# Patch embedding in token rows: pixels stationary, weights moving, in a fused embedding, attention and feed-forward kernel

## The reference

```
h = patches(x) @ W_embed + b_embed + pos_embed      # 196 x 256 for each image
h = concatenate([h, txt], axis=1)                   # 228 x 256
h = h + attention(layernorm(h))                     # 16 heads of 16, causal, then @ Wo.T + bo
h = h + ffn(layernorm(h))                           # ternary up 256 -> 1024, gelu, ternary down
```

## Time and profile before

| what | before |
|---|---|
| median of three runs | 2072.05 us |
| the profiled execution | 2070.54 us |
| its span in the profile | 2068.8 us |
| mean granted clock of TensorE | 0.978 |
| TensorE busy | 94% of the span |
| VectorE, ScalarE, GpSimd busy | 73%, 63%, 43% |

### The profile page before, as it was taken

How to read it: one execution, slowest core, us unless ns; L and a number is a source line. 1 busy time by engine, 2 the same in 40 slices (tenths; PEclk the granted TensorE clock), 3 DMA queues, 4 the chain that set the end, 5 groups by cost and what they waited for, 6 DMA issues and landing times.

```text
span 2068.8 us, 61840 instructions
## 1 busy us (share of the span) xinstructions
PE 1939.4 (94%) x25986; PEld 1574.5 (76%) x25986; DVE 1514.4 (73%) x2849; ACT 1296.2 (63%) x2050; POOL 887.8 (43%) x1069
## 2 busy tenths in 40 slices
PE   2889999999999999999999999999999999999875
PEld 2668788778778777777877877887787787777664
DVE  5457778778777777777877777787777777777753
ACT  2346666666666666666666666666666666666652
POOL 1124444444444544443444444444444445444443
PEclk8789999999999999999999999999999999999987
DMA  4111111011111101111111111110111111010000
GB/s 133 26 44 40 50 53 49 29 49 40 53 49 53 48 26 49 44 50 52 49 40 39 44 49 49 54 49 28 50 40 53 49 54 46 28 49 22 29 29 23
DMA packets 62989, 93.85 MB, mean 45 GB/s; under 512 B 9634, under 2 KB 59270, under 8 KB 59768
## 3 DMA queue, kind: packets, MB, share of 16 engines
q1 hardware_dynamic: 62712, 89.90, 15.7%
HBM read 45.03 MB, written 14.94 MB: 29 GB/s over the span
## 4 chain that ended last, share of the span: by engine, by line
PE 71%; DVE 20%; issue 4%; ACT 3%; POOL 1%; DMA 1%; DVEq 0%; SPq 0%; POOLq 0%; ACTq 0%
PE dense L327 41%; PE score L327 17%; PE pvps L327 7%; PE dense L384 2%; DVE st L942 2%; DVE rs L914 2%; DVE mx L954 2%; DVE km L990 2%; PE dense L345 2%; DVE h L938 2%; DVE pT_lo L904 2%; PE dense L373 2%; DVE h L1030 1%; DVE mr L966 1%; DVE aT_lo L908 1%
## 5 line engine op out<-in xcount | busy, mean ns | idle before, releaser
L1161 POOL TENSOR_SCALAR_AFFINE_SELECT pr<-pr 114x456 f32<-114x456 f32 x512 | 311.9, 634 | 899.9 <-ACT pr L668 899.9
L668 ACT ACTIVATE pr<-score 114x1368 f32<-114x1368 f32 x256 | 335.7, 1311 | 302.2 <-PE score L327 301.9
L953 DVE TENSOR_REDUCE mx<-score 114x4 f32<-114x456 f32 x256 | 161.4, 630 | 187.3 <-PE score L327 187.1
L954 DVE TENSOR_REDUCE mx<-score 114x4 f32<-114x912 f32 x256 | 281.1, 1098 | 0.0
L327 PE MATMUL dense<-wdn,g 128*114 128x256 bf16 x1024 | 241.0, 281 | 3.5 <-issue 3.5
L1180 POOL TENSOR_TENSOR acc<-acc,sq 128x456 f32<-128x456 f32 x192 | 229.2, 1194 | 18.9 <-POOL acc L1180 0.4
L327 PE MATMUL dense<-wdn,gl 128*114 128x256 bf16 x1024 | 235.1, 275 | 0.0
L327 PE MATMUL score<-km,qs 32*114 32x114 f32 (+1 forms) x4096 | 221.7, 331 | 7.8 <-ACT pr L668 7.6
L327 PE MATMUL pvps<-pr,vp 114*32 114x228 f32 (+1 forms) x4096 | 204.6, 317 | 0.5 <-ACT raw L740 0.5
L914 DVE RECIPROCAL rs<-rs 128x228 f32<-128x228 f32 x128 | 200.8, 1568 | 0.0
L327 PE MATMUL score<-qs,km 32*114 32x228 f32 (+1 forms) x4096 | 196.4, 308 | 0.0
(11 more groups left out here) (135 smaller groups left out, 4423.4 us busy)
## 6 DMA issues: line engine op xcount, KB each, us to landing
pix<-x SPq DMA_DIRECT2D x32, 1176.0 KB
rs<-raw SPq DMA_DIRECT2D x256, 57.0 KB, 2.0
cx<-raw SPq DMA_DIRECT2D x256, 57.0 KB, 2.0
out<-h SPq DMA_DIRECT2D x64, 228.0 KB
h<-txt SPq DMA_DIRECT2D x32, 64.0 KB, 8.0
km<-wqkvo SPq DMA_DIRECT2D x1, 1024.0 KB, 15.4
h<-w_upT SPq DMA_DIRECT2D x1, 1024.0 KB, 14.5
km<-w_embed SPq DMA_DIRECT2D x1, 768.0 KB, 10.3
```

The lines of the kernel that those rows point to most:

```text
L668: act(pr[q % 2][:], score[0:R, :, 0:SW], ACT.Exp, scale=float(HD) ** -0.5).then_inc(a["exp"], 1)
L953: nc.vector.tensor_reduce(mx[:, b, 0, :, r], score[0:R, :, 0:R], AX.X, ALU.max)
L954: nc.vector.tensor_reduce(mx[:, b, 1, :, r], score[0:R, :, R:SW], AX.X, ALU.max).then_inc(v["max"], 1)
L1161: nc.gpsimd.affine_select(out=blocks, in_=blocks, compare_op=ALU.is_ge, fill=0.0, base=0, pattern=[[0, 4], [1, R]], channel_multiplier=-1) ...
```

## The change

The pixels become the stationary operand and the weights the moving one. `embed(pair, blk, ph)` now works on a block of token rows: for each image `b` and each colour it loads 114 (block 0) or 82 (block 1) patches of `pT` as stationary columns and moves 256 columns of `we`. The result has tokens in the partitions already. `hidden_columns`, the tile `hT`, `hidden_rows` and the semaphores `pe["emb"]` and `a["emb"]` are gone. `("ht", 0)` and `("ht", 1)` take the places of `("emb", 0)` and `("emb", 1)` in `DENSE`; the old places of `ht` and the spare place are gone. `embed(t, 1, 1)` moves from the end of stage 3 to stage 4, where `hidden_rows` stood. `hidden(t, hs, 0)` moves on VectorE from stage 4 to stage 2, behind the two `lo_part`.

```diff
-         ("pix", 5), ("emb", 0), ("x2t", 0), ("x2t", 1), ("up", 0), ("up", 1), ("up", 2), ("up", 3), ("up", 4),
-         ("up", 5), ("up", 6), ("up", 7), ("emb", 1), ("ht", 0), ("ht", 1), ("v", 1), ("mt", 0), ("spare", 0), ("dn", 0),
+         ("pix", 5), ("ht", 0), ("x2t", 0), ("x2t", 1), ("up", 0), ("up", 1), ("up", 2), ("up", 3), ("up", 4),
+         ("up", 5), ("up", 6), ("up", 7), ("ht", 1), ("v", 1), ("mt", 0), ("dn", 0),
...
-            def embed(pair, m, ph):
+            def embed(pair, blk, ph):
...
-                    eng.wait_ge(*emptied(pair, "emb", m))
+                    eng.wait_ge(*emptied(pair, "ht", blk))
                 eng.wait_ge(v["pix"], count(6, pair, 3 * ph + 3))
-                o = bank_of("emb", m)[:, 0:TP].rearrange("p (b n) -> p b n", b=2)
-                for c in range(C):
-                    mov = [q[:, ph].rearrange("p (b c n) -> p b c n", b=2, c=C)[:, :, c] for q in pT]
-                    stat = [w[:, 2 * c + ph, m * 128:m * 128 + 128] for w in we]
-                    last = three(o, stat, mov, ph == 0 and c == 0, ph == 1 and c == 2)
-                if ph == 1:
-                    last.then_inc(pe["emb"], 1)
-
-            def hidden_rows(pair, blk):
...
                 w = R if blk == 0 else RP1
                 for b in range(2):
-                    for m in range(2):
-                        c0 = b * NPATCH + blk * R
-                        last = nc.tensor.transpose(ps[0:w, b * D + m * 128:b * D + m * 128 + 128],
-                                                   hT[:, m, c0:c0 + w], ident[:])
-                last.then_inc(pe["ht"], 1)
+                    o = bank_of("ht", blk)[0:w, b * D:b * D + D]
+                    for c in range(C):
+                        n0 = (b * C + c) * NPATCH + blk * R
+                        last = three(o, [q[:, ph, n0:n0 + w] for q in pT], [z[:, 2 * c + ph] for z in we],
+                                     ph == 0 and c == 0 and b == 0, ph == 1 and c == 2,
+                                     skip_group_check=True)
+                if ph == 1:
+                    last.then_inc(pe["ht"], 1)
...
                     if A and k == 4:
-                        hidden_rows(t, 0)
-                        hidden_rows(t, 1)
+                        embed(t, 1, 1)
...
                     if A and k == 3:
                         embed(t, 1, 0)
-                        embed(t, 1, 1)
...
                     if began(pair - 1):
-                        eng.wait_ge(pe["emb"], count(2, pair - 1, 2))
+                        eng.wait_ge(pe["ht"], count(2, pair - 1, 2))
...
-                    if A and k == 2:
-                        hidden_columns(t, 0)
...
-                    if A and k == 4:
-                        hidden_columns(t, 1)
...
+                    if A and k == 2:
+                        hidden(t, hs, 0)
                     if A and k == 4:
-                        hidden(t, hs, 0)
                         hidden(t, hs, 1)
```

More of the change, by code:

```diff
@@ L59 @@
 DENSE = [("o", 0), ("o", 1), ("pix", 0), ("pix", 1), ("pix", 2), ("mt", 1), ("v", 0), ("pix", 3), ("pix", 4),
[2 rows of a table removed]
[2 rows of a table added]
          ("dn", 1), ("ss", 0), ("xt", 0), ("xt", 1), ("qk", 0), ("qk", 1), ("qk", 2), ("qk", 3)]
-PER = {"pix": 6, "emb": 2, "up": 8, "o": 2, "ht": 2, "xt": 2, "qk": 4, "v": 2, "ss": 1,
+PER = {"pix": 6, "up": 8, "o": 2, "ht": 2, "xt": 2, "qk": 4, "v": 2, "ss": 1,
        "dn": 2, "x2t": 2, "mt": 2}
-LAG = {"pix": 0, "emb": 0, "ht": 0, "xt": 0, "qk": 0, "v": 1, "o": 3, "x2t": 3, "up": 3,
+LAG = {"pix": 0, "ht": 0, "xt": 0, "qk": 0, "v": 1, "o": 3, "x2t": 3, "up": 3,
        "ss": 3, "dn": 3}
@@ L102, in build @@
         pT = [sb("pT_hi", [128, 2, 2 * C * NPATCH], F32R), sb("pT_lo", [128, 2, 2 * C * NPATCH], F32R)]
-        hT = sb("hT", [128, 2, TP], F32)
         h = sb("h", [128, 4, 4 * D], F32)
@@ L167, in build @@
         s_apart = sem("s_apart")
-        pe = {n: sem("pe_" + n) for n in ["pix", "emb", "ht", "xt", "qk", "v", "s", "st", "pv", "mt",
+        pe = {n: sem("pe_" + n) for n in ["pix", "ht", "xt", "qk", "v", "s", "st", "pv", "mt",
                                           "o", "x2t", "up", "ss", "dn", "init"]}
-        a = {n: sem("a_" + n) for n in ["ro", "pix", "emb", "xt", "q", "v0", "exp", "mt", "raw", "km",
+        a = {n: sem("a_" + n) for n in ["ro", "pix", "xt", "q", "v0", "exp", "mt", "raw", "km",
                                         "ct", "x2t", "gelu", "sq", "w", "xn", "xn2"]}
@@ L193, in apart @@
             eng.sem_inc(s_apart, 1)
-        released = {"pix": v["pix"], "emb": a["emb"], "ht": v["h"], "xt": v["xt"],
+        released = {"pix": v["pix"], "ht": v["h"], "xt": v["xt"],
                     "v": a["v0"], "o": v["h2"], "x2t": v["x2t"], "up": a["gelu"],
@@ L327, in mm, with three @@
                 return nc.tensor.matmul(*args, **kw)
[L329 to L333, removed]
+            def three(ps, stat, mov, start, stop, **kw):
+                mm(ps, stat[0], mov[0], start=start, stop=False, **kw)
+                mm(ps, stat[0], mov[1], start=False, stop=False, **kw)
+                return mm(ps, stat[1], mov[0], start=False, stop=stop, **kw)
             eng.wait_ge(p["w"], 9)
@@ L347, in pixels @@
                 last.then_inc(pe["pix"], 1)
-            def embed(pair, m, ph):
-                if isinstance(pair, int) and pair == 0 and m == 0 and ph == 0:
+            def embed(pair, blk, ph):
+                if isinstance(pair, int) and pair == 0 and blk == 0 and ph == 0:
                     eng.wait_ge(v["we"], 1)
                 if ph == 0:
-                    eng.wait_ge(*emptied(pair, "emb", m))
+                    eng.wait_ge(*emptied(pair, "ht", blk))
                 eng.wait_ge(v["pix"], count(6, pair, 3 * ph + 3))
-                o = bank_of("emb", m)[:, 0:TP].rearrange("p (b n) -> p b n", b=2)
-                for c in range(C):
-                    mov = [q[:, ph].rearrange("p (b c n) -> p b c n", b=2, c=C)[:, :, c] for q in pT]
-                    stat = [w[:, 2 * c + ph, m * 128:m * 128 + 128] for w in we]
-                    last = three(o, stat, mov, ph == 0 and c == 0, ph == 1 and c == 2)
-                if ph == 1:
-                    last.then_inc(pe["emb"], 1)
-            def hidden_rows(pair, blk):
[L365 to L368, removed]
                 w = R if blk == 0 else RP1
                 for b in range(2):
-                    for m in range(2):
-                        c0 = b * NPATCH + blk * R
-                        last = nc.tensor.transpose(ps[0:w, b * D + m * 128:b * D + m * 128 + 128],
-                                                   hT[:, m, c0:c0 + w], ident[:])
-                last.then_inc(pe["ht"], 1)
+                    o = bank_of("ht", blk)[0:w, b * D:b * D + D]
[6 more added lines that the diff above has]
+                    last.then_inc(pe["ht"], 1)
             def to_columns(pair, name, m, src):
@@ L740, in unscaled @@
                 act(raw[:, k % 2].rearrange("p y s -> p (y s)"), pvps[:, 0:T2], ACT.Copy).then_inc(a["raw"], 1)
[L742 to L746, removed]
             reorder(0, 0)
```

## The result

The changed kernel took 2124.61 us in the median of four runs (2122.63 to 2129.03), the kernel before 2072.44 (four runs). The ratio is 1.0256, 95% interval 1.024 to 1.0272: 52 us slower. 2123 was forecast. The profiled execution took 2124.62 us with a span of 2122.8, against 2068.8 before. The mean granted clock is 0.979, before 0.978, so the clock has no part in it.

What follows compares the result with a forecast made beforehand. TensorE was taken to bound the kernel, busy 59.68 of 60.84 us a step. 1.24 us in 32 steps (39.7) plus 0.43 in 29 (12.5), together 52.2 on 2070.54, gave 2122.7, rounded to 2123; range 2106 to 2138.

Steps and rivals of the forecast that it cites:

- TensorE sets the step, and added work adds: Stages 1 to 5: each microsecond added to TensorE is a microsecond of the step; nothing is waited for there.
- The stream: Four embedding groups of 18 matmuls at 0.119 us, 9.04 us a step against 7.80: 1.24 us added in 32 steps.
- Loads behind the matmuls: Embedding groups: weight loads, doubled from 36 to 72 a step, overlap and cost nothing; uncovered, 4.1 us a step.
- ScalarE's relief is worth nothing: Stages 2 and 4: two dropped copies of 0.50 us gain nothing, except x2t's high part 0.05 us sooner.
- The wait at `up`: Stage 2: first up matmul waits for position add behind low parts on VectorE, 0.43 us in 29 steps, 12.5 us.
- rival A: Stage 2: the wait of `up` for `hidden` doesn't show, if high parts came 0.4 us sooner; 2110 us, chance 0.13.
- The exponential's cover: Stage 3: cover before stage 4's score rows shrinks from 1.16 to 0.07 us; costed at nothing, at most 0.1 a step.
- The sum: Whole kernel: 39.7 us in 32 steps plus 12.5 us in 29 steps, together 52.2, on 2070.54: 2122.7, rounded to 2123.
- B: Embedding groups: 256 f32 columns take 0.107 us, near one a cycle, 0.86 us a step less; 2095 us, chance 0.06.
- C: Late exponential, slower `hidden` or showing loads: 0.4 us more a step, 2136 us; all loads showing, 2254; chance 0.15.
- D: Round through VectorE, ScalarE and `hT` sets the step, not TensorE: up to 1.0 us a step faster, 2039 us, chance 0.04.
- E: No change: the added work falls into TensorE waits of the same size in the step; 2072 us, chance 0.02.

Runs made afterwards that it cites:

- f16 runs: High and low parts of pixels and embedding weights in f16 instead of f32: in the kernel before 2060.24 us, in the changed kernel with position add first 2090.47 us.
- kernel with the add first: The changed kernel with block 0's position add on VectorE in stage 2 ahead of the two low parts of x2t instead of behind them: 2110.68 us.
- one with two products: The changed kernel with the position add first, and the product of high pixels and low weights left out of the embedding: 2062.16 us.

## Why the prediction was right

**TensorE sets the step, and added work adds.** Right. A usual step is 1.63 us longer, of which 0.52 are the new wait, by the run that undid it, and 1.11 the stream. One reading was not right: that nothing is waited for in stages 1 to 5. The list of waits leaves out the short ones, and two of them, some 0.09 and 0.08 us, stood ahead of `up` and of the first down matmul.

**The stream.** Right in mechanism, 0.13 us a step too high. The spacing of 0.119 us measured 0.118, so the groups came out at 2.31, 2.22, 2.31 and 2.17 against 2.33, 2.24, 2.33 and 2.14. With the values, which lost their opening, the five groups take 10.51 us against 7.80 + 1.59 = 9.39 before, 1.12 more, where I had added 1.24. Of this 0.12, 0.09 is the opening: I left it in the values' 1.59 us and let their 12 matmuls cost as before, but they got 0.09 shorter. The other 0.03 are in the four groups. The step differs by 1.11 and not by 1.12 because two smaller things nearly cancel: the 0.08 us ahead of the first down matmul that went away, and pieces of 0.02 us and less in other stages. (The prediction's second account, 2.16 more in matmuls less 0.85, is 1.31 and not 1.24: the openings and gaps around the groups, 7.80 - 0.85 - 6.41 = 0.54 us before and 0.47 after, are missing from it.) By the Trainium skill's formula for one matmul by itself (page "TensorE: Matmul & The Clock Gate", section "Back-to-back issue gap") 256 columns would be 109 ns apart and 392 166. The f16 runs show 166 for 392, in agreement; the f32 parts of this kernel don't follow it, with 118 and 178.

**Loads behind the matmuls.** Right: 176 ns loads at a spacing of 118, and 30 wider loads moved the step by 0.04 us.

**ScalarE's relief is worth nothing.** Right as to its load, by the copies put back. The 0.05 us by which the high part of `x2t` should have come sooner did not come: it starts 0.65 us after the transposes (1068.32 against 1067.67), as before (0.64).

**The wait at `up`.** Right in place and cause. From the transposes to `up`, start to start, 3.06 us pass (1067.67 to 1070.73) where 2.55 did (1095.78 to 1098.33), so `up` is 0.51 late; the list books 0.53. 0.43 was forecast. The difference is the 0.05 above, 0.01 in the add's end (0.60 behind the low parts) and 0.02 in the handover (0.06). The 0.15 us called cover in the prediction, and in its rival A, was none, as shown above. The sum holds all the same, because `up` did start 0.15 us behind the low parts before, and only lateness against that start counts.

**The exponential's cover.** Right in place, and nearly in size: 0.07 us of cover were forecast, none were left, and TensorE stands about 0.06 us, within the bound of 0.1. Taking six matmuls from the group ahead turned all of their 0.70 us into waiting at once.

**The sum.** 32 x 1.11 + 29 x 0.53 = 50.9 us, where the spans differ by 54.0. The rest, 3 us, lies outside the usual steps, mostly in single steps that are longer than the others: over 28 steps they add 4.6 us in the changed kernel's one profiled execution and 0.9 in the kernel before. What makes them long wasn't found. So the terms were off by +4.2 and -2.9, and what was not in the sum brought 3. The last step of the prediction is off too: 52.2 on the median of 2072.05 gives 2124.2, and it wrote 2123. That this came within 2 us of the median, with errors that cancel, is partly luck.

**The rivals.** A: the wait does show. B: the f32 stream runs at 0.118 us for 256 columns and not at 0.107. C: loads do not show, and of the cover ahead of the exponential only 0.06 us a step was overdrawn. D and E: the step got longer, so neither the round through `hT` nor idle time of the same size took up the added work.

## What to carry to other kernels

When TensorE sets the step, compare two orientations by the columns they move, pieces with few stationary columns counted in full: here 18,432 against 14,112, and a transpose back of 0.85 us was the cheaper way. When a bank gets another reader, ask where in the reader's queue the release stands; one exchange of two neighbours on VectorE was worth 14 us. And count what a shorter stream will find: of 2.80 us taken from TensorE in a step, 1.34 arrived, because one cover was used up already, and another went to a pair of VectorE instructions that took 1.88 us longer. A wait too short for the list shows itself in the distance from start to start, by comparison with the same matmuls elsewhere in the step.

## What the runs showed that I had not expected

VectorE's two low parts of gelu (128x456, f32 to f16, all operands in SBUF) in stage 4 take 1.16 us with no sum of squares on GpSimd alongside. With sums alongside they took 3.04 in one kernel, where three sums took 4.41, and 1.16 in another, where the three sums took 4.75. One sum by itself took 1.16. So both engines, or one of them, lose time when they meet, and a shift of 0.7 us in where they meet decides which. The single sums show more. In the kernel with the add first (its third sum) and in the one with two products (its second):

```profile
1076.66 2.13 POOL L1158 TENSOR_TENSOR acc<-acc,sq 128x456 f32<-128x456 f32 x1
```

```profile
1106.12 1.59 POOL L1159 TENSOR_TENSOR acc<-acc,sq 128x456 f32<-128x456 f32 x1
```

In the first, VectorE's pair started at 1076.61, 0.05 us ahead of the sum, and it was the sum that took 2.13 us instead of 1.16, while both low parts kept their 0.62. In the second the sum was already running when the pair started at 1106.66, and the first low part took 1.53 us; there the sum took longer as well, 1.59. So in both it was the instruction that started second that lost most, 0.97 and 0.91 us. The changed kernel has the first case: its third sum takes 2.13 us in 28 steps, which makes nearly all of GpSimd's 28.3 us more busy time than in the earlier trace rows, and TensorE doesn't wait for it. No run here moved the two engines' starts alone. The Trainium skill, page "GPSIMD Engine Reference", section "1. Specifications", names contention of the two engines for SBUF when a VectorE instruction has two SBUF inputs, and the low parts have two. The traces agree that they hold each other up: 1.88 us fell on the VectorE pair in one kernel and nothing in the other. That the order of the starts decides it is read from these traces and was not tested.
